# Source one-hots of the edge stage: number row in PSUM, and their place in VectorE's order behind the products

## The reference, cut to what matters

```python
Q = (x @ Wq).reshape(N, 8, 32); K = (x @ Wk).reshape(N, 8, 32); V = (x @ Wv).reshape(N, 8, 32)
score = (Q[src] * K[tgt]).sum(axis=-1) * scale + edge_attr @ We     # 53125 edges x 8 heads
m = segment_max(score, tgt); ex = exp(score - m[tgt]); den = segment_sum(ex, tgt)
out = segment_sum((ex / den[tgt])[:, :, None] * V[tgt], tgt).reshape(N, 256) @ Wo + bo
```

## Time and profile before

| what | value |
|---|---|
| median of 3 runs | 2576.47 us |
| the profiled execution, its span | 2554.21 us, 2552.4 us |
| edge stage: first to last reduction or product on VectorE | 139.12 to 849.67 us |
| VectorE busy between 195 and 799 us | 335.67 us of 604 us |
| TensorE matmul busy between 195 and 799 us | 440.04 us |
| GpSimd busy between 195 and 799 us | 362.30 us |
| TensorE clock granted between 195 and 799 us | 0.66 of full speed |
| DMA engines' mean busy share between 195 and 799 us | 0.42 |

### The profile page before, as it was taken

One profiled execution on the slowest core, in us unless ns is written; L12 is line 12 of the kernel. 1 busy time (PEld: TensorE's weight loads), 2 busy tenths in 40 slices (PEclk: granted clock), 3 DMA queues, 4 the chain that ended last, 5 costly groups with the idle time before them and its releaser, 6 DMA issues. The chain is left out here.

```text
span 2552.4 us, 39948 instructions
## 1 busy us (share of the span) xinstructions
PE 1968.1 (77%) x12472; PEld 1615.8 (63%) x12473; DVE 1308.3 (51%) x2763; ACT 878.2 (34%) x1815; POOL 1177.6 (46%) x1170
## 2 busy tenths in 40 slices
PE   6536677777777769969934888888885869999996
PEld 4424455555555557758733666766764768999896
DVE  7215555555556844335656666776763682222221
ACT  4314434444435324432223121221212463333332
POOL 2665556555654030015556555555664004444443
PEclk9857756666667869989976888998997959999998
DMA  3584444444444616346665655554554247677675
GB/s 80 148 195 119 111 117 121 117 114 115 120 119 109 130 33 165 111 135 203 213 174 167 202 181 168 173 175 161 172 176 134 76 149 207 199 190 197 185 198 152
DMA packets 203090, 383.59 MB, mean 150 GB/s; under 512 B 43381, under 2 KB 138026, under 8 KB 202767
## 3 DMA queue, kind: packets, MB, share of 16 engines
q1 hardware_dynamic: 136871, 223.77, 29.1%
q0 software_dynamic: 65264, 156.19, 22.9%
q10 hardware_dynamic: 840, 2.16, 0.3%
HBM read 276.75 MB, written 108.69 MB: 151 GB/s over the span
## 5 line engine op out<-in xcount | busy, mean ns | idle before, releaser
L808 POOL DMA_INDIRECT qr<-q_rows,src_t x415 | 415.5, 1001 | 271.5 <-DVE dots L1014 156.3
L2323 PE MATMUL psP<-f_part,onehot 125*128 125x256 bf16 x3600 | 464.7, 290 | 76.4 <-issue 62.0
L906 PE MATMUL psK<-kp,oh_k 126*128 x1680 | 344.6, 367 | 185.2 <-DVE qr L1011 91.6
L2303 POOL DMA_INDIRECT fr<-pair_rows,dst_i x372 | 357.7, 961 | 252.8 <-DVEq L2365 147.5
L2323 PEld LDWEIGHTS psP<-f_part,onehot 125*128 125x128 bf16 x3600 | 370.5, 104 | 160.6 <-issue 86.1
L906 PEld LDWEIGHTS psK<-kp,oh_k 126*128 126x128 bf16 x1680 | 204.9, 124 | 300.6 <-issue 228.8
L1011 DVE TENSOR_TENSOR qr<-qr,psK 128x512 f32<-128x512 f32 (+1 forms) x252 | 141.0, 592 | 316.9 <-remote 195.3
L2361 DVE SCALAR_TENSOR_TENSOR psA<-psA,same,fr 128x256 f32<-128x256 f32 x420 | 206.4, 492 | 153.8 <-ACT fr L2439 123.6
L1919 ACT ACTIVATE m1hT<-m1psH,m1par 128x128 f32<-128x128 f32 x448 | 128.1, 368 | 253.2 <-issue 133.6
L1939 PEld LDWEIGHTS m1psH<-m1xT,n_rows 128*128 128x128 f32 x1792 | 208.7, 192 | 3.9 <-DMA n_rows<-in_L_ffn_W_dram 1.1
L1939 PE MATMUL m1psH<-m1xT,n_rows 128*128 128x128 f32 x1792 | 209.2, 275 | 0.9 <-DMA n_rows<-in_L_ffn_W_dram 0.9
(11 more groups left out here) (502 smaller groups left out, 2844.2 us busy)
## 6 DMA issues: line engine op xcount, KB each, us to landing
n_rows<-in_L_ffn_W_dram SPq DMA_DIRECT2D x56, 1024.0 KB
run_rows<-acc SPq DMA_DIRECT2D x84, 640.0 KB
loc<-locals_ SPq DMA_DIRECT2D x85, 157.5 KB
ea<-in_edge_attr_dram SPq DMA_DIRECT2D x84, 140.0 KB
w_first<-in_L_ffn_Wd_dram SPq DMA_DIRECT2D x8, 1024.0 KB, 11.8
w_all<-in_L_ffn_W_dram SPq DMA_DIRECT2D x8, 1024.0 KB, 10.1
m1b<-in_L_ffn_b_dram SPq DMA_DIRECT2D x56, 128.0 KB
qr<-q_rows,src_t POOLq DMA_INDIRECT x420
```

Of the source, the lines that this page charges most:

```text
L808: nc.gpsimd.indirect_dma_start(out=qr[:, n % GQ, u, :], out_offset=None, in_=q_rows, in_offset=bass.IndirectOffsetOnAxis(ap=src_t[:, n, u: ...
L906: last = nc.tensor.matmul(psK[:, m, (u - a) * D:(u - a + 1) * D], oh_k[:, K_SLOT[g], c, u * E:(u + 1) * E], kp[:, bass.ds(first[u] + c, 1) ...
L2303: nc.gpsimd.indirect_dma_start(out=fr[:, n % GI, u, :], out_offset=None, in_=f_rows, in_offset=bass.IndirectOffsetOnAxis(ap=f_at[:, n * G ...
L2323: last = nc.tensor.matmul(psP[:, k % 2, 0:D], onehot[:, k % 2, t, :], f_part[:, c, t, :], start=(t == 0 and c == 0), stop=(t == T - 1 and ...
```

## The change

The numbers 0 to 124 are copied once from `iota_row` into columns 256 to 380 of the third bank of `psK`, which the expansion doesn't use. The comparisons read them there. VectorE makes the source one-hots of group n + 1 between the products and the reduction of group n; those of group 0 come ahead of the loop. The third bank is read by these comparisons, so the signal that it is free again comes no longer from the third product, but from an increment of its own behind the one-hots, which waits for them. The reduction waits on a new semaphore, `s_multiplied`, that the third product counts up.

```diff
+        s_multiplied = sem1("rows_multiplied")
+            iota_ps = psK[0:E, 2, D:D + P]
-                v.sem_inc(s_kfree, 3)
+                v.sem_inc(s_kfree, 2)
+                dve_order.link(v, nc.vector.tensor_copy(iota_ps, iota_row[:]))
+
+                def source_onehots(n):
+
+                    g, at = n % GI, slice(n * G, (n + 1) * G)
+                    v.wait_ge(s_ohu, n + 1)
+                    nc.vector.tensor_tensor(oh_lo[:, g], iota_ps.unsqueeze(1).to_broadcast([E, G, P]),
+                                            lo[:, at].unsqueeze(2).to_broadcast([E, G, P]), ALU.is_equal)
+                    nc.vector.tensor_tensor(oh_hi[:, g], iota_ps[:, 0:T].unsqueeze(1).to_broadcast([E, G, T]),
+                                            hi[:, at].unsqueeze(2).to_broadcast([E, G, T]), ALU.is_equal).then_inc(s_oh, 1)
+                    v.wait_ge(s_oh, n + 1)
+                    v.sem_inc(s_kfree, 1)
+
                 k_onehots(0, K_SLOT[0], 0)
+                source_onehots(0)
                 for n in range(NK):
...
                     k_onehots((n + 1) % GI, K_SLOT[(n + 1) % GI], (n + 1) // GI)
-                    v.wait_ge(s_ohu, n + 1)
-                    nc.vector.tensor_tensor(oh_lo[:, g], iota_row[:]...)
-                    nc.vector.tensor_tensor(oh_hi[:, g], iota_row[:, 0:T]...).then_inc(s_oh, 1)
                     v.wait_ge(s_got[n % GQ], G * 16 * (n // GQ + 1))
                     for m, (a, b) in enumerate(BANKS):
                         v.wait_ge(s_kx, n * 3 + m + 1)
-                        nc.vector.tensor_tensor(row[:, a:b]..., psK[:, m, 0:(b - a) * D], ALU.mult).then_inc(s_kfree, 1)
-                    v.wait_ge(s_kfree, n * 3 + 6)
+                        last = nc.vector.tensor_tensor(row[:, a:b]..., psK[:, m, 0:(b - a) * D], ALU.mult)
+                        if m < len(BANKS) - 1:
+                            last.then_inc(s_kfree, 1)
+                        else:
+                            last.then_inc(s_multiplied, 1)
+                    if n + 1 < NK:
+                        source_onehots(n + 1)
+                    v.wait_ge(s_multiplied, n + 1)
                     nc.vector.tensor_reduce(dots[:, :, at]..., ALU.add).then_inc(s_free, 1)
```

More of the change, by code:

```diff
@@ L997, in _ @@
                 v.sem_inc(s_kt, GI)
-                v.sem_inc(s_kfree, 3)
+                v.sem_inc(s_kfree, 2)
[9 more added lines that the diff above has]
+                    v.sem_inc(s_kfree, 1)
                 k_onehots(0, K_SLOT[0], 0)
+                source_onehots(0)
                 for n in range(NK):
-                    g, row, at = n % GI, qr[:, n % GQ], slice(n * G, (n + 1) * G)
+                    row, at = qr[:, n % GQ], slice(n * G, (n + 1) * G)
                     k_onehots((n + 1) % GI, K_SLOT[(n + 1) % GI], (n + 1) // GI)
-                    v.wait_ge(s_ohu, n + 1)
[L1004 to L1007, removed]
                     v.wait_ge(s_got[n % GQ], G * 16 * (n // GQ + 1))
@@ L1010, in _ @@
                         v.wait_ge(s_kx, n * 3 + m + 1)
-                        nc.vector.tensor_tensor(row[:, a:b].rearrange("p u d -> p (u d)"), row[:, a:b].rearrange("p u d -> p (u d)"),
-                                                psK[:, m, 0:(b - a) * D], ALU.mult).then_inc(s_kfree, 1)
-                    v.wait_ge(s_kfree, n * 3 + 6)
+                        last = nc.vector.tensor_tensor(row[:, a:b].rearrange("p u d -> p (u d)"), row[:, a:b].rearrange("p u d -> p (u d)"),
+                                                       psK[:, m, 0:(b - a) * D], ALU.mult)
+                        if m < len(BANKS) - 1:
[5 more added lines that the diff above has]
+                    v.wait_ge(s_multiplied, n + 1)
                     nc.vector.tensor_reduce(dots[:, :, at].rearrange("p h u -> p u h"),
```

## The result

| | before | changed |
|---|---|---|
| median, lowest to highest | 2573.59 us, 2570.23 to 2580.61 (4 runs) | 2606.4 us, 2605.24 to 2620.66 (4 runs) |
| ratio, 95% interval | | 1.0144, 1.0116 to 1.0173 |
| profiled execution, its span | 2554.21 us, 2552.4 us | 2606.15 us, 2604.4 us |
| end of the last reduction | 849.67 us | 899.2 us |

The changed kernel is slower: by 33 us between the medians, by 37 us by the ratio (0.0144 x 2574). The direction was forecast and the median lies in the range. In the two profiled executions nearly all of the difference is in the edge stage: its end moved by 49.5 us, the executions differ by 51.9.

What follows compares the result with a forecast made beforehand. Edge stage bound by TensorE's signals held behind ten gathers' traffic, then VectorE's products and reduction before GpSimd restarts. 36.1 - 12.4 + 0.5 = 24.2 us on 2576.5 gave 2601 us, range 2570 to 2617.

Steps and rivals of the forecast that it cites:

- The gap is paid at each restart: VectorE's reduction starts 0.95 us later, delaying GpSimd's restart each time: 38 x 0.95 = 36.1 us.
- The operand in PSUM is worth nothing: VectorE's source comparisons reading PSUM instead of SBUF were taken at the present 1.00 us: no change.
- The long gather is worth nothing: GpSimd's fifth gather of a stretch may fall from 1.42 to 0.95 us; this was given nothing.
- The release stays 14.8 us behind the restart: TensorE's held signals are out once ten gathers' traffic drains; `score` still fetched 14.8 us after GpSimd's restart.
- What comes back: TensorE, not waiting for the reduction, starts ahead of GpSimd's restart, shortening 20 stretches: 12.4 us taken back.
- rival 1: Nothing comes back, as bank 3 holds TensorE up wherever it gained its lead: 36.6 us, 2613 us; chance 0.17.
- Bank 3 comes free later: The third `psK` bank is freed 1.0 us later, but TensorE reaches it only afterwards: not late.
- The end of the stage: Behind the last gather VectorE sets the pace for nine groups; one more wait of 0.06 us each: 0.5 us.

Runs made afterwards that it cites:

- order only: Kernel before, with source one-hots moved between products and reduction, still reading SBUF, third product freeing its bank, no wait for their end: 2575.69 us, 1.0091.
- third bank on time: Changed kernel with comparisons reading SBUF and the third product itself freeing the third bank again: 2606.5 us, 1.0218.
- spare pair: Kernel before plus a second, useless pair of comparisons and a wait for it between products and reduction: 2576.83 us, 1.0091.
- batch without held signals: Runs where the kernel before took 2202.06 us and TensorE's signals came promptly; the change with comparisons reading SBUF measured 0.9990 there.
- behind the reduction: Changed kernel with the source one-hots of group n + 1 moved behind the reduction of n: 2595.17 us, 1.0167.
- batch 3: Runs with held signals: before 2548.84 us, the unmodified changed kernel 2596.15 us, the change with comparisons reading SBUF 2597.15 us.
- change again: The changed kernel, unmodified, measured a second time against the kernel before: 2596.15 us, 1.0179.
- batch 4: Runs with before at 2549.0 us: the change reading SBUF with its third bank freed by the product 2606.5 us; before with GpSimd paced by TensorE 2513.87 us.

## Why the prediction was right, and where it was off

The direction and its cause were right; the size was low because of one term, and the range covered that.

- **The gap is paid at each restart: right.** It is 1.07 us, 1.04 more than before, where I had 0.95 (0.15 us pass between the end of the second comparison and the reduction; I had 0.06). With 39 waits that is 40.6 us against 36.1. The two comparisons make 0.83 us of it (order only), the wait for their end 0.12 (third bank on time, 0.96), the increment that frees the third bank 0.11. That stretches of one class grow by 0.99 us here, by 0.84 and 0.85 with the spare pair's gap of 0.96, and that the batch without held signals loses nothing (0.999, same gap) show that it is paid, and where.
- **The operand in PSUM is worth nothing: right.** 0.80 us in both and 0.28 against 0.30; 2596.15 against 2597.15 us.
- **The long gather is worth nothing: right**, to 0.1 us a stretch (behind the reduction), and it went for another reason than the operand.
- **The release stays 14.8 us behind the restart: right**, 14.80. The reading under it, that the signals are out when the traffic has drained, is only roughly so. Before, the traffic of the stretch in the earlier trace rows ends 0.3 us ahead of the release, 14.2 us behind the restart. In the changed kernel the fifth gather is shorter and the traffic ends 13.8 us behind the restart, but the release stays at 14.4; this is the stretch shown above, columns as in the earlier trace rows:

```profile
641.50:642.10 0.60, 0.00 (x0) 0.00 (x0) 0.00 (x0) 0.00 (x0) 0.00 (x0) 0.50 0.00 0
```

- **"What comes back": this step failed.** From TensorE's starting ahead of the restart I took 12.4 us back. TensorE now does so in 34 of 35 stretches, as forecast, and 33 of them have the length of the class with one early bank, 18.23 us, which is 17.24 + 0.99. The 16 early-starting stretches of before were shorter because two or three bank signals came early in 15 of them. The early start went along with that and isn't enough for it: within the class of two, 12 early starters and 7 late ones all last 16.58 to 16.76 us. With this term at nothing the sum is rival 1 in its number: 36.6 us, or 2613 us and a ratio of 1.0142. Measured: 1.0144. That they agree so closely is partly luck. With the gap as measured the sum is 40.6 + 1.0 = 41.6 us, a ratio of 1.0162, still within the interval; and the same kernel gave 1.0179 in batch 3. Rival 1's reason, that bank 3 holds TensorE up, isn't shown either: "third bank on time" is no faster.
- **Bank 3 comes free later, "not late": right**, shown by "third bank on time", which gains nothing.
- **The end of the stage:** from the last restart to the last reduction it takes 50.6 us before (799.08 to 849.7) and 52.6 after (846.57 to 899.2). 1.04 of the 2.0 us is the gap of that stretch; 1.0 us is left, where 0.5 was forecast.
- **The profiled pair differs by more than the runs.** Its mean stretch grew by 1.44 us: 1.04 for the gap, and 0.40 because 22 of 36 stretches of before had more than one early bank and 1 of 35 of the changed kernel. By the medians (33 us) the second part hardly shows; the timed runs of before were 16 us and more above its profiled one. In batch 3 it may show: 47 us with the change again; batch 4's 58 us are those of "third bank on time".

**What stays open.** Why every form of the change that keeps its order locks into one early bank, while "order only" and the spare pair do not. The operand and the third bank are excluded, the third bank by kernels of different batches (3 and 4). The wait for the one-hots' end is the only line between "order only" and "third bank on time", but the spare pair has such a wait too, and these kernels ran in different batches, so it isn't shown to be the cause; a run of both in one batch would tell.

## What to carry to other kernels

Ask of each moved instruction whether the engine that restarts the next round waits behind it: 1 us ahead of a reduction that releases the gathers cost 1 us in each of 39 restarts, and nothing in a batch where nobody waited for it. A property that goes along with short rounds in a trace (here: TensorE's early start) is no lever until an experiment moves it alone. Where results are there and their news is not, try what comes of issuing fewer gathers at a time; here it gave 1.5%, about what the change cost.

## What the hardware showed that I had not expected

- The last of TensorE's signals came through 14.2 to 14.8 us behind the start of a burst of ten gathers of 128 x 1 KB, and 7.6 us behind that of one of five.
- The signals that come earlier don't come at any time. Products of early banks start near 5.87 us behind the restart or whole steps of 0.71 us from there: 58 of 61 before and 36 of 36 in the changed kernel to within 0.13 us, where chance would put about a third (8.78 and 13.05 us in the stretches shown). What makes the step no run tells.
- The same kernel took 2202 us in one batch and 2549 to 2574 us in four others. In the fast one hardly any signal was held, though the DMA engines were busier there (0.58 against 0.42).
- A gather's 0.95 us grew to 1.42 us or 1.62 us where it started 0.2 us after a VectorE comparison of two SBUF operands had begun, to 1.28 us at 0.55 us, and hardly at 0.7 us; starting first, it kept 0.96 us. The comparison took 0.80 to 0.83 us in every case.
- Two executions of one kernel had 3 and 11 short stretches, with means of 16.77 and 16.31 us over the stretches of ten, and the stage's end 8 us apart. A term of 12 us taken from such classes in one profile is of the size of that scatter.
